# Two scatters, one gelu and four copies change their stage, and two loop heads change their order

## The chip, the cores and the metric

The kernel runs on one core of a Trainium2 chip. A core has five engines that run their own instruction streams and meet only at semaphores: TensorE (PE: matmuls), VectorE (DVE), ScalarE (ACT: activation functions and copies), GpSimd (POOL) and SyncE (SP: it issues DMA transfers). The metric is device time in microseconds (us), the median over several runs.

## The reference, cut to what matters

The reference is a transformer of two layers over 4 x 512 tokens of 128 channels. The part that matters is the attention of the first layer, with 16 heads and a window of 64 keys that slides over time:

```python
strain = disp_win - disp[:, :, :, None, :]             # 64 window places per token
bond_act = gelu(strain @ W_strain + rel_emb @ W_pos)   # exact gelu
damage_act = gelu(strain @ W_dmg + b_dmg)
logits = bond_act @ W_bond - 10.0 * sigmoid(damage_act @ W_dmg_out + b_dmg_out)
weights = softmax(where(cmask, logits, -inf))
out = einsum("bntd,bntde->bnte", weights, val_win)     # then W_cproj
```

Beside it stands a mixture of 16 experts of which each token uses 4: x + attention(xn) + experts(xn). The second layer (ordinary attention and 8 experts) is not touched by the change.

## The kernel before, in words

The first layer runs in five blocks, one after another: set-up, then for each of two groups of 8 heads (g = 0, 1) a loop and a band stage. At the end of a block all engines wait for each other.

**The loop.** It goes through the 64 window places j as items, eight to a body (`it`). For an item VectorE writes two halves, s = 0 (bond) and s = 1 (damage), into one of four ring slots (`strained`, line 261). For the items 1, 2, 4, 5 and 7 of a body TensorE makes the s = 1 half instead, in two half passes (`strain`, lines 999 and 1003) from `DS`, a copy of the data in three bfloat16 parts; ScalarE then takes the gelu of such an item in three pieces (lines 921, 922 and 924), of the others in one (line 916). TensorE reduces the gelus into logits (`reduce`, line 975), which frees the ring slot. Beside this run the experts' groups, four tiles of 128 rows each: SP loads rows (`tokens`) and weights, TensorE turns them and multiplies (`turn`, `hidden`, `expert_out`), VectorE moves and activates (`move_in`, `glu_in`, `glu_out`, `move_out`), and GpSimd scatters the results to DRAM with four indirect transfers a group (`store`, line 267). `MOE` says which groups a body handles: in the first loop groups 0 to 4, in its bodies 5, 6 and 7; in the second loop the other fifteen, in its bodies 0 to 7.

**The head of the first loop.** TensorE counts the tokens of each expert (`count`, `starts`), VectorE makes the tables (`expert_tiles`, `token_slots`, `tile_tables`), GpSimd scatters 64 sets of rows to the experts' order (line 770). The copies into `DS` (`send_parts`, line 256) are four transfers for each of three parts; parts 0 and 1 are sent by SP in set-up, part 2 in the loop.

**The band stage.** TensorE turns the logits, VectorE subtracts the maxima, ScalarE takes the exp, SP writes the result to DRAM (`band`), and SP and GpSimd read it back skewed, one half of the partitions each (`read`, line 1168), into three buffers (`wide`) that GpSimd clears first (line 1176). It clears `vp`, too, the tile for the values (line 1177). TensorE then turns and gathers what was read, for four blocks k of time steps. In the first band stage the other head group's data are prepared beside it, among them item 0 of the second loop (`strained` by VectorE in block 3), whose gelu opens the second loop.

What sets the order is each engine's own program, written out by hand; the semaphores only say how long it waits.

Of the kernel before, what the change touches and what calls it, by code (L numbers as in the profile page):

```python
# [20 lines left out]
P = 128  # L21
B, T, C = 4, 512, 128
NT = T // P
# [64 lines left out]
def first_step(j):  # L88

    return WIN - 4 - 4 * (j // 4)  # L90
# [91 lines left out]
def first_layer(nc, t_in, l0, sb, psum, sem, ident, ACC, nhalf, stats, mv, rstd, carried):  # L182
# [87 lines left out]
    with ExitStack() as su:  # L270
# [49 lines left out]
        def _(sp):  # L320
# [25 lines left out]
            send_parts(sp, 0, parts0, (1,))  # L346
# [293 lines left out]
    wide_zero, side_pe, side_sb = sem("wide_zero"), sem("side_pe"), sem("side_sb")  # L640
# [26 lines left out]
    for g in range(G):  # L667
        with ExitStack() as lp:
# [21 lines left out]
            def _(sp):  # L690
# [25 lines left out]
                if g == 0:  # L716
                    send_parts(sp, 0, parts0, (2,))
# [26 lines left out]
            def _(pool):  # L744
# [28 lines left out]
                for n in groups:  # L773
                    if n < groups[-1]:
                        goals(n + 1)
                    pool.wait_ge(goals_ready, n + 1)
                    if g or n < groups[-1]:
                        store(pool, n)

            @block.vector  # L780
            def _(v):
# [104 lines left out]
                if g == 0:  # L886
                    v.wait_ge(items_reduced, 1)
                    strain(0, 0, 0)
                    expert_tiles()
                    strain(0, 0, 1).then_inc(strain_ready, 1)  # L890
                    token_slots()
                item(1, 0)
                if g == 0:
                    tile_tables()
                item(2, 0)
# [9 lines left out]
            def _(act):  # L905
# [50 lines left out]
                gelu(0, 0)  # L956
# [5 lines left out]
            def _(pe):  # L962
                def reduce(n, it):
# [9 lines left out]
                    for s in range(2):  # L973
# [3 lines left out]
                    mm.then_inc(items_reduced, 1)  # L977
# [109 lines left out]
                strain(1, 0, 0)  # L1087
                if g == 0:
                    tables()
                strain(1, 0, 1)  # L1090
                reduce(0, 0)
                turn(moe_groups(g, 0)[0])
                strain(2, 0, 0)
# [9 lines left out]
        with ExitStack() as sm:  # L1103
# [52 lines left out]
            def read(engine, k, half, only=None):  # L1156

                engine.wait_ge(wide_zero, (WIDE + 1) * g + min(k, WIDE - 1) + 1)
# [13 lines left out]
            def _(pool):  # L1172
                if g == 0:
                    store(pool, MOE[0][7][1])
                for n in range(WIDE):
                    pool.memset(wide[n], 0.0).then_inc(wide_zero, 1)
                pool.memset(vp, 0.0).then_inc(wide_zero, 1)
                for k in range(NT):
                    read(pool, k, 1)
# [36 lines left out]
            def _(v):  # L1216
# [41 lines left out]
                for k in range(NT):  # L1258
# [7 lines left out]
                    if (g, k) == (0, 3):  # L1266
                        strained(v, ring[:, 0], 0, 1)
# [12 lines left out]
            def _(act):  # L1280
# [33 lines left out]

                weigh(0)
# [3 lines left out]
                act.wait_ge(wide_zero, (WIDE + 1) * (g + 1))  # L1319
                values(0)  # L1320
                for k in range(NT):
# [12 lines left out]
                    for i in sides(k)[1]:  # L1334
                        side(i)

# [1137 lines left out]
```

## Time and profile before

| | |
|---|---|
| time, median of 3 runs | 1234.41 us (1232.6 to 1237.3) |
| the profiled execution | 1235.36 us, its span 1233.6 us |
| set-up | 0 to 46.3 us |
| first loop, first band stage | 46.3 to 312.9, 312.9 to 395.0 us |
| second loop, second band stage | 395.0 to 655.9, 655.9 to about 750 us |
| busy over the span | PE 82%, DVE 73%, ACT 63%, POOL 45% |

All times of a row are us from the first instruction of the execution. A row of the timeline gives start, duration, engine, line, operation, what it writes and reads, and in brackets how long the engine stood idle before it and whose end released it. "issue" is a wait for nothing that the profile shows; "PEq" is a sequencer. An engine that is not the last to arrive at a point can be idle at no cost.

### The profile page before, as it was taken

What the parts mean: (1) busy time and instruction counts of PE and PEld (TensorE: products, weight loads), DVE (VectorE), ACT (ScalarE), POOL (GpSimd) and SP (SyncE); (2) the same over time, 40 slices, a digit from 0 to 9 for tenths busy, and PEclk for the clock granted to TensorE, in tenths of its full rate; (3) what the DMA queues carried; (4) which work ended last, traced back from release to release, by engine and by line L of the source; (5) the groups of instructions that cost most, each with busy time, mean ns of one, the idle gap of its engine ahead of it and who ended that gap; (6) DMA issues with size and microseconds to landing.
All of it is one profiled execution on the core that took longest, in us unless ns stands there. A gap on an engine that the chain in (4) does not pass through costs nothing. (4 is left out here: it accounts for less than half of the span.)

```text
span 1233.6 us, 24798 instructions
## 1 busy us (share of the span) xinstructions
PE 1016.2 (82%) x9866; PEld 547.7 (44%) x9866; DVE 894.7 (73%) x1046; ACT 783.0 (63%) x848; POOL 550.8 (45%) x571
## 2 busy tenths in 40 slices
PE   6687777898587988988885879987799999998557
PEld 4422222233566333333334868345345656464123
DVE  7778788997637899999986555684485776667137
ACT  3589999998544899999995322421465665555234
POOL 5188887067734188888876104057300000000720
PEclk9789999999799999999998889987699999899679
DMA  8840111021493122222206910002113435231110
GB/s 298 246 154 33 35 35 35 19 64 41 121 235 73 49 73 71 71 69 68 69 31 188 257 40 22 0 10 92 37 52 111 129 113 154 77 86 52 50 28 26
DMA packets 117418, 105.32 MB, mean 85 GB/s; under 512 B 11861, under 2 KB 103665, under 8 KB 116657
## 3 DMA queue, kind: packets, MB, share of 16 engines
q1 hardware_dynamic: 107220, 83.41, 24.1%
q0 software_dynamic: 8512, 20.13, 5.6%
q8 instruction: 78, 1.28, 0.4%
q10 hardware_dynamic: 1571, 0.20, 0.1%
q14 instruction: 37, 0.30, 0.1%
HBM read 62.16 MB, written 38.39 MB: 82 GB/s over the span
## 5 line engine op out<-in xcount | busy, mean ns | idle before, releaser
L261 DVE SCALAR_TENSOR_TENSOR ring<-AD,PT 128x1808 f32<-128x1808 f32 (+15 forms) x128 | 282.8, 2222 | 35.0 <-PE LG L975 20.2
L975 PE MATMUL LG<-ring,lred 128*32 128x456 f32 (+15 forms) x2048 | 238.5, 586 | 0.0
L2240 ACT ACTIVATE EX<-SS 128x1024 f32<-128x1024 f32 x128 | 130.8, 1030 | 122.7 <-PE SS L2027 80.0
L267 POOL DMA_INDIRECT ys<-rows,goali x80 | 160.8, 2010 | 106.9 <-DVE rows L861 76.1
L2310 DVE TENSOR_REDUCE MX<-SS 128x2 f32<-128x1024 f32 x119 | 144.5, 1218 | 71.7 <-PE SS L2027 50.5
L916 ACT ACTIVATE ring<-ring 128x3616 f32<-128x3616 f32 (+15 forms) x48 | 164.4, 3424 | 3.7 <-DVE ring L261 3.6
L999 PE MATMUL SD<-DSf,eyes 99*32 99x456 bf16 (+15 forms) x1280 | 95.9, 376 | 78.0 <-ACT ring L921 69.7
L922 ACT ACTIVATE ring<-ring 128x1824 f32<-128x1824 f32 (+15 forms) x80 | 145.7, 1821 | 0.0
L1944 POOL DMA_INDIRECT XN<-ys,sloti x16 | 16.6, 1040 | 269.3 <-PE SS L2037 264.7
L770 POOL DMA_INDIRECT xs<-rows,sloti x64 | 122.1, 1907 | 30.2 <-issue 19.2
L975 PEld LDWEIGHTS LG<-ring,lred 128*32 128x32 f32 x2048 | 61.8, 112 | 100.6 <-issue 78.8
L261 DVE SCALAR_TENSOR_TENSOR ring<-AD,bdmg 128x1808 f32<-128x1808 f32 (+15 forms) x48 | 106.4, 2217 | 0.0
L999 PEld LDWEIGHTS SD<-DSf,eyes 99*32 99x32 bf16 x1280 | 21.2, 95 | 179.8 <-ACT ring L921 111.6
L921 ACT ACTIVATE ring<-SD 128x912 f32<-128x912 f32 (+15 forms) x80 | 78.3, 979 | 30.3 <-PE SD L1003 17.4
L1003 PE MATMUL SD<-DSf,eyes 96*32 96x456 bf16 (+15 forms) x1280 | 95.4, 374 | 0.0
L2027 PE MATMUL SS<-QS,KS 32*128 32x512 f32 x256 | 67.8, 530 | 28.1 <-ACT EX L2240 21.1
L924 ACT ACTIVATE ring<-SD 128x912 f32<-128x912 f32 (+15 forms) x80 | 78.5, 981 | 10.0 <-PE SD L1003 9.9
L2027 PE MATMUL SS<-KS,QS 32*128 32x512 f32 x238 | 63.2, 518 | 14.5 <-DVE MX L2310 12.5
L2047 PE MATMUL PW<-EX,VA 128*32 128x512 f32 x512 | 73.4, 649 | 0.0
L2217 ACT ACTIVATE HB<-PHh,b1c 128x128 f32<-128x128 f32 x156 | 44.7, 371 | 41.3 <-PE PHh L1979 41.3
L2362 DVE RECIPROCAL attT<-attT 128x128 f32<-128x128 f32 (+1 forms) x58 | 54.5, 959 | 0.2
L2027 PEld LDWEIGHTS SS<-QS,KS 32*128 32x128 f32 x256 | 25.3, 195 | 64.0 <-ACT EX L2240 30.9
(417 smaller groups left out, 1751.1 us busy)
## 6 DMA issues: line engine op xcount, KB each, us to landing
w1s<-in_L_ffn_W SPq DMA_DIRECT2D x39, 256.0 KB
w2s<-in_L_ffn_W SPq DMA_DIRECT2D x39, 256.0 KB
band<-ring SPq DMA_DIRECT2D x6, 1024.0 KB, 9.5
xl<-xs SPq DMA_DIRECT2D x20, 272.0 KB, 3.1
xs<-Z SPq DMA_DIRECT2D x5, 1024.0 KB, 8.5
w1s<-w1d SPq DMA_DIRECT2D x80, 64.0 KB
w2s<-w2d SPq DMA_DIRECT2D x80, 64.0 KB
band<-Z SPq DMA_DIRECT2D x4, 1024.0 KB
```

Of the source, the lines that this page charges most:

```text
L261: return v.scalar_tensor_tensor(out=tile[:, s, :, t0:T], in0=AD[:, s, :, j + t0:j + T], scalar=extra, in1=AD[:, s, :, PAD + t0:PAD + T], o ...
L267: pool.indirect_dma_start(ys0[:, :], bass.IndirectOffsetOnAxis(ap=goali[:, 4 * n + a:4 * n + a + 1], axis=0), yo[:, n % 2, a, :], None, bo ...
L770: pool.indirect_dma_start(xs0[:, :], bass.IndirectOffsetOnAxis(ap=sloti[:, t, k:k + 1], axis=0), rows[:, t, :], None, bounds_check=ROWS0 - ...
L916: act.activation(tiles, tiles, ACT.Gelu).then_inc(gelu_done, 1)
L922: act.activation(tiles, tiles, ACT.Gelu)
L924: act.activation(ring[:, slot, 1, 2:4, t0:T], SD[:, :, t0:T], ACT.Gelu).then_inc(gelu_done, 1)
L975: mm = pe.matmul(LG[32 * b:32 * b + 32, par, s, t0:T], lred[:, s, n % 4, :], ring[:, slot, s, b, t0:T], start=(n % 4 == 0), stop=(n % 4 == 3))
L999: pe.matmul(SD[32 * q:32 * q + 32, i, t0:T], eyes[0:99, q, :], DS[0:99, q, 2 * half + i, j + t0:j + T], start=True, stop=False)
L1003: mm = pe.matmul(SD[32 * q:32 * q + 32, i, t0:T], eyes[0:96, 4, :], DS[0:96, q, 2 * half + i, PAD + t0:PAD + T], start=False, stop=True)
L2027: mm = pe.matmul(bank[:, n, :], rows[r:r + 32, b % 2, q, P * t:P * t + P], cols[r:r + 32, b % 2, q, :], start=True, stop=True)
L2240: act.activation(EX[:, Q % 2, hh:hh + 2, t, :], SS[:, slot, :, :], ACT.Exp, scale=SCALE1).then_inc(freed[slot], 1)
L2310: v.tensor_reduce(MX[:, t, p // 2, hh:hh + 2], pairs_of(b, name), AX.X, ALU.max).then_inc(freed[slot], 1)
```

## The change: what it does

- `send_parts` for part 1 goes from SP's set-up to SP's first loop, beside part 2.
- The head of the first loop: VectorE computes item 1 ahead of `token_slots`, and item 2 ahead of `tile_tables`. TensorE puts `tables` behind the second half of item 1's strain, and the reduction of item 0 behind the first half of item 2's.
- The first loop's last two scatters (groups 3 and 4; of these group 4's was in the band stage already) both stand in the first band stage, each behind one clear; the clear of the third buffer and the later reads come after them. The clear of `vp` goes to ScalarE as a copy of a zero column, ahead of its exps, in both band stages.
- The gelu of the second loop's item 0 is done at the end of the first band stage by ScalarE, in two pieces (s = 1, then s = 0); VectorE signals the first piece by a semaphore of its own.
- The head of the second loop: TensorE splits the reduction of item 0 in two (s = 0 before, s = 1 behind the second half of item 1's strain), and turns the experts' rows behind the first half of item 2's strain.

```diff
@@ set-up, SP
-            send_parts(sp, 0, parts0, (1,))
@@ first loop, SP
-                    send_parts(sp, 0, parts0, (2,))
+                    send_parts(sp, 0, parts0, (1, 2))
@@ loops, GpSimd
-                    if g or n < groups[-1]:
+                    if g or n < groups[-2]:
                         store(pool, n)
@@ loops, VectorE
-                    token_slots()
                 item(1, 0)
                 if g == 0:
+                    token_slots()
+                item(2, 0)
+                if g == 0:
                     tile_tables()
-                item(2, 0)
@@ loops, ScalarE
-                gelu(0, 0)
+                if g == 0:
+                    gelu(0, 0)
                 gelu(1, 0)
@@ loops, TensorE
-                def reduce(n, it):
+                def reduce(n, it, which=(0, 1)):
...
-                    for s in range(2):
+                    for s in which:
...
-                    mm.then_inc(items_reduced, 1)
+                    if which[-1]:
+                        mm.then_inc(items_reduced, 1)
...
                 strain(1, 0, 0)
+                if g:
+                    reduce(0, 0, (0,))
+                strain(1, 0, 1)
+                if g:
+                    reduce(0, 0, (1,))
+                else:
+                    tables()
+                strain(2, 0, 0)
                 if g == 0:
-                    tables()
-                strain(1, 0, 1)
-                reduce(0, 0)
+                    reduce(0, 0)
                 turn(moe_groups(g, 0)[0])
-                strain(2, 0, 0)
                 strain(2, 0, 1)
@@ band stages, GpSimd
+                def clear(n):
+                    pool.memset(wide[n], 0.0).then_inc(wide_zero, 1)
+
+                clear(0)
+                if g == 0:
+                    store(pool, MOE[0][7][0])
+                clear(1)
+                read(pool, 0, 1)
                 if g == 0:
                     store(pool, MOE[0][7][1])
-                for n in range(WIDE):
-                    pool.memset(wide[n], 0.0).then_inc(wide_zero, 1)
-                pool.memset(vp, 0.0).then_inc(wide_zero, 1)
-                for k in range(NT):
+                clear(2)
+                for k in range(1, NT):
                     read(pool, k, 1)
@@ band stages, VectorE
-                        strained(v, ring[:, 0], 0, 1)
+                        strained(v, ring[:, 0], 0, 1).then_inc(parts_dve, 1)
@@ band stages, ScalarE
+                act.copy(vp.rearrange("p a n h e -> p (a n h e)"), xnT[:, 0, 0:1].to_broadcast([P, 2 * 8 * HG * 32])).then_inc(vp_zero, 1)
                 weigh(0)
...
-                act.wait_ge(wide_zero, (WIDE + 1) * (g + 1))
+                act.wait_ge(vp_zero, g + 1)
...
+                if g == 0:
+                    for s, ready, count, done in ((1, parts_dve, 5, parts_act), (0, strain_ready, 65, gelu_done)):
+                        tiles = ring[:, 0, s, :, first_step(0):T]
+                        act.wait_ge(ready, count)
+                        act.activation(tiles, tiles, ACT.Gelu).then_inc(done, 1)
```

## Rows read from the trace of the kernel before

**Rows 1.** Busy time by stretch: start:end, length, PE, PEld, DVE, ACT, POOL, PE clock.

```profile
46.30:69.50 23.20, 17.83 (x168) 10.80 (x168) 17.95 (x36) 11.18 (x9) 11.47 (x15) 0.74 1.04 327
69.50:299.00 229.50, 188.66 (x2252) 66.49 (x2252) 196.50 (x127) 215.85 (x155) 160.16 (x109) 0.97 0.13 41
...
410.50:653.00 242.50, 215.52 (x2508) 89.85 (x2504) 226.39 (x201) 226.20 (x169) 185.96 (x151) 1.00 0.21 62
```

**Rows 2.** VectorE's waits in the second loop: us in total, times, longest.

```profile
DVE rows L861 <- PE PY L1054: 8.1, 8, 2.4
```

**Rows 3.** Timeline, set-up into the first loop: start, us, instruction, idle before.

```profile
41.08 4.55 SPq L256 DMA_DIRECT2D DSf<-tT  x4
...
46.33 2.10 DVE L261 SCALAR_TENSOR_TENSOR ring<-AD,PT 128x1808 f32<-128x1808 f32 x1 [2.99 <-PEq L270]
...
46.36 2.68 SPq L256 DMA_DIRECT2D DSf<-XN  x4
```

**Rows 4.** Timeline, the edges behind the loops and into the second loop.

```profile
293.92 2.55 POOL L267 DMA_INDIRECT ys<-rows,goali  x1 [0.30 <-issue]
...
305.10 0.97 POOL L267 DMA_INDIRECT ys<-rows,goali  x1 [0.30 <-issue]
...
312.96 1.23 DVE L1218 TENSOR_TENSOR Z<-Z,mz 128x1024 f32<-128x1024 f32 x1 [4.95 <-PEq L668]
...
395.03 6.13 DVE L261 SCALAR_TENSOR_TENSOR ring<-AD,PT 128x1808 f32<-128x1808 f32 x3 [0.32 <-PEq L1103]
...
649.72 0.98 POOL L267 DMA_INDIRECT ys<-rows,goali  x1 [0.31 <-issue]
...
655.93 1.23 DVE L1218 TENSOR_TENSOR Z<-Z,mz 128x1024 f32<-128x1024 f32 x1 [2.65 <-PEq L668]
```

**Rows 5.** Timeline, head of the first loop.

```profile
51.22 3.22 ACT L916 ACTIVATE ring<-ring 128x3616 f32<-128x3616 f32 x1 [3.65 <-DVE ring L261]
...
54.87 0.42 DVE L817 SCALAR_TENSOR_TENSOR chosen_key<-PH,chosen_key 128x256 f32<-128x256 f32 x1 [3.68 <-PE PH L1023]
...
55.16 0.56 PE L1003 MATMUL SD<-DSf,eyes 96*32 96x452 bf16 x8
...
59.84 0.93 ACT L921 ACTIVATE ring<-SD 128x904 f32<-128x904 f32 x1 [5.41 <-DVE ring L261]
...
60.66 1.71 ACT L922 ACTIVATE ring<-ring 128x1808 f32<-128x1808 f32 x1
...
62.31 3.06 PE L975 MATMUL LG<-ring,lred 128*32 128x452 f32 x16
...
68.02 1.69 PE L975 MATMUL LG<-ring,lred 128*32 128x452 f32 x16
...
69.48 3.22 ACT L916 ACTIVATE ring<-ring 128x3616 f32<-128x3616 f32 x1
```

**Rows 6.** Timeline, first band stage.

```profile
318.86 3.53 POOL L1176 MEMSET ring<- 128x4096 f32 x1
...
319.16 2.05 ACT L1287 ACTIVATE ring<-wtT 128x1024 f32<-128x1024 f32 x1 [4.95 <-issue]
...
336.18 1.17 POOL L1168 DMA_DIRECT2D DSf<-band  x2 [1.13 <-DMA band<-ring]
...
357.56 1.11 PE L1384 MATMUL WB<-ident,DSf 128*128 128x128 f32 x8
...
389.96 2.10 DVE L261 SCALAR_TENSOR_TENSOR ring<-AD,PT 128x1808 f32<-128x1808 f32 x1
```

**Rows 7.** A scatter in the first loop; the four in the band stage, grouped.

```profile
61.24 7.79 POOL L770 DMA_INDIRECT xs<-rows,sloti  x1 [0.31 <-issue]
...
L267 POOL DMA_INDIRECT ys<-rows,goali x4 | 4.3, 1074 | 8.5 <-POOLq L668 7.6 <-issue 0.9
```

**Rows 8.** Transfers of 333 to 353 us: count, KB each, us to landing.

```profile
DSf<-band POOLq DMA_DIRECT2D x2, 380.0 KB, 9.4
```

**Rows 9.** Timeline, head of the second loop.

```profile
410.81 2.12 DVE L261 SCALAR_TENSOR_TENSOR ring<-AD,PT 128x1824 f32<-128x1824 f32 x1 [1.94 <-PE LG L975]
```

More of the change, by code:

```diff
@@ L639, in first_layer @@
         sem(n) for n in ("band_pe", "band_act", "band_dve", "vw_pe", "vw_sb", "nd_pe", "rc_ready", "att_ready"))
-    wide_zero, side_pe, side_sb = sem("wide_zero"), sem("side_pe"), sem("side_sb")
+    wide_zero, vp_zero, side_pe, side_sb = sem("wide_zero"), sem("vp_zero"), sem("side_pe"), sem("side_sb")
     def fetch(sp, k):
@@ L1156, in read @@
             def read(engine, k, half, only=None):
-                engine.wait_ge(wide_zero, (WIDE + 1) * g + min(k, WIDE - 1) + 1)
+                engine.wait_ge(wide_zero, WIDE * g + min(k, WIDE - 1) + 1)
                 if k >= WIDE:
```

## The prediction, made before the changed kernel ran

> **What bounds the kernel now.** I read the split of the span by stage first, then who waits for whom inside the two loops, then the timeline around each edge between stages. In the first loop's steady part ScalarE is busy 215.85 of 229.5 us, VectorE 196.5; in the second loop's 226.20 and 226.39 of 242.5, and of VectorE's 16 us without work 8.1 are waits for the expert outputs on TensorE [rows 1, 2]. So the first loop ends when ScalarE's row of gelus ends, the second when VectorE's or ScalarE's does: work that hides elsewhere is worth nothing, and what such a loop can be given is an earlier start. The change touches exactly the starts: two heads and two edges. The timeline shows how much is idle there.
>
> **Edge from set-up into the first loop.** VectorE stood idle 2.99 us before its first instruction at 46.33, while SP issued the four copies of the second part until 45.63 (41.08 + 4.55) [rows 3]. With the copies moved behind the edge, VectorE is last, with its end at 43.34. How fast an edge is when nothing holds it shows at the one into the second loop: VectorE idle 0.32 us [rows 4]; from SP's end to 46.33 it is 0.70. The edge falls at 43.7 to 44.0: 2.3 to 2.6 us won. The copies are not gone: SP now issues eight in a row, at 0.67 us each (46.36: 2.68 for four) to 1.14 (41.08) [rows 3]: 5.4 to 9.1 us. TensorE's first strain matmuls, which wait for them, end at 55.72 and start about 1 us earlier, behind the counting of tokens [rows 5], 8.4 us after the edge. Their cover is that counting. At 0.67 us each 3.0 us remain for landing, at 1.14 they are 0.7 us late plus the landing, which no row gives alone; so the term lies between 0 and 2.6. The 1.14 belongs to copies that queue behind set-up's weight transfers; these get 2.7 us more, so I take the nearer row, 0.67, and **2.3**. The zero stores and expert weights behind them on SP move by about as much; the expert groups begin in the sixth body, over 100 us later.
>
> **Head of the first loop.** ScalarE ends its first gelu at 54.44, then idles 5.41 us before the second item's first piece; the first gelu in one piece after that, item 3's, starts at 69.48 [rows 5]. The 5.41 us are a wait for VectorE's item 1, which stands behind the token slots, for which VectorE itself idled 3.68 us (before 54.87). In the new order item 1 (2.1 us, the mean of three in 6.13 us [rows 4]) runs in that gap, 51.2 to 53.3. Then, in the clock of before: strain matmuls until 55.72; gelu 1's first half 0.93 us until 56.7; second strain half about 1.0 until 57.7; ScalarE's other two pieces 1.7 and 0.93 until 59.3; strain of item 2 until 60.3, its first half gelu until 61.2; the delayed first reduction (1.69 us at the full clock, row 68.02) until 62.0, second strain half until 63.0, gelu 2 ends 63.9. VectorE: token slots end at 57.7 as before (item 1 now ends behind them at 59.8), item 2 59.8, tables 60.3, item 3 (two pieces) 64.4. So gelu 3 starts at 64.4 in place of 69.48: 5.1 us. The doubt is TensorE's clock: its granted mean in this head is 0.74 against 0.97 behind it [rows 1], and the same reduction took 3.06 us at 62.31, behind two idle stretches of some 2.1 us: there it ran at 1.2 in place of 2.4 GHz. Were all these matmuls at the lower level, the same walk gives 66.8, thus 2.7. The new gaps are each 1.1 us or less, so the full clock is nearer: **4.6**, between 2.7 and 5.1.
>
> **Edge out of the first loop.** VectorE idles 4.95 us before the band stage, from 308.01 [rows 4]. GpSimd's last scatter ended at 306.07 (305.10 + 0.97), 6.9 us before. At the end of the second loop, where its last scatter ended at 650.70, 5.2 us before, the idle time is 2.65. At the edge into the second loop, with no scatter near, it is 0.32. I read it as GpSimd arriving 5 to 7 us after a scatter. In the new kernel the last scatters before this edge are group 2's, which end at 296.5, 11.5 us before 308.01. Then VectorE is last: 4.95 less 0.32 to 0.70 gives 4.2 to 4.6, **4.4**; below, 0, if something else holds the edge.
>
> **Band stage.** Three things are added. ScalarE clears the value tile (128 x 4096) in GpSimd's place: the gelu of 3,616 elements took 3.22 us [rows 5], so 3.7; ScalarE's first exp waits until 319.16, 6.2 us into the stage, of which its wait for VectorE is the last 4.95 [rows 6]. Cost 0, cover 1.2 us even if what stands before that wait stays. ScalarE's moved gelu is two pieces of 1.7 us, the second after VectorE's strain piece at 392.06 (389.96 + 2.10); it ends near 393.9, before VectorE's last piece at 394.7 [rows 4, 6]: cost 0, cover 0.8. GpSimd's order becomes clear, scatters, clear, first read, scatters, clear, reads. A scatter there takes 1.07 us on average, a group with its issue gaps 5.2 [rows 7]. The first read, behind 3.5 + 5.2 + 3.5 = 12.2 us, is earlier than now (behind two more clears); the second, now issued at 336.18, 23.3 into the stage, falls at 23.3 to 25. It needs 9.4 us to land [rows 8] and TensorE turns it at 357.56: 10 us of cover. **0**.
>
> The price of a scatter is the place where the stage could turn. A scatter in the first loop took 7.79 us at 61.24 [rows 7], across VectorE's unbroken row of strain pieces. The Trainium skill, "SBUF — State Buffer", section "SBUF: two separate sides", says that a VectorE operation with two inputs in SBUF and a GpSimd operation that reads SBUF exclude each other for the whole instruction. By that rule the 7.79 belongs to the strain pieces, the band stage's reductions and subtractions, which read PSUM, would not stretch a scatter, and the term stays 0; the 1.07 agrees. Without it a busy DMA queue would be the other reading, the one priced in the last rival.
>
> **Head of the second loop.** VectorE's item 5 starts at 410.81, 15.8 us into the stage, after 1.94 us of waiting for TensorE's reduction 1 [rows 9]; ScalarE's gelu 1 stands behind gelu 0. With gelu 0 done, ScalarE starts on gelu 1 when item 1 is there (395.03 + 2.05 = 397.1): its pieces until 398.0, 399.7, 400.7; strain of item 2 until 401.9; gelu 2's pieces 402.8, 404.5, 405.4; gelu 3 at 405.4. Reduction 1 follows the second strain half (404.0) and ends 405.7: item 5 at 405.9 in place of 410.81, 4.9 us. At the lower clock gelu 3 starts at 406.8 and item 5 at 409.1, 1.7 earlier. VectorE is as full as ScalarE here [rows 1], so its figure counts. Half of the reduction of item 0 now stands in one of TensorE's gaps, none over 1.1 us; I take **4.2**.
>
> **Sum.** 2.3 + 4.6 + 4.4 + 0 + 4.2 = 15.5 us. The profiled execution took 1235.36 (its span 1233.6 and 1.76 around it), 0.95 above the median of the runs: 1219.9 against it, 1218.9 against the median 1234.41. That is the forecast. Its own bounds: least 0 + 2.7 + 4.2 + 1.7 = 8.6 (1225.8), most 2.6 + 5.1 + 4.6 + 4.9 = 17.2 (1217.2).
>
> **Rivals.** (a) The edge out of the first loop keeps its 4.95 us, since not GpSimd holds it. For: TensorE's side also idles there, and the last scatter's 64 KB cannot take 6 us to move. Against: the two edges of rows 4 that are slow are the two with a scatter 5 to 7 us before, and the idle times shrink together. Time 1218.9 + 4.4 = 1223.3. The Trainium skill, "DMA: Bandwidth & Descriptors", section "Anatomy of one DMA — SWDGE (gpsimd) path", gives about 2.0 us fixed per GpSimd transfer, mostly the write's receipt. By that figure, as an estimate, GpSimd would be done near VectorE's end at 308, which speaks for (a); the 6.9 us of the row speaks against its being all.
> (b) The loops hand the heads back: a later meeting with expert weights or GpSimd's queue sets their end. For: the 8.1 us of waits for expert outputs [rows 2]. Against: those waits hang on work that itself moves with the loop. Time: only the edges count, 6.7 us, 1227.7.
> (c) Slower: a scatter in the band stage stretches to the 7.79 us of row 61.24. Eight of them put 8 x 6.7 = 54 us before the second read, less its 10 us of cover: 44 us at TensorE's turns, net 1263. It decides from a stretch of 15.5 + 10 = 25.5 us on, 4.3 us a scatter. Against: the 1.07 us of four in this stage.
>
> **How the numbers follow.** Forecast 0.66, (a) 0.14, (b) 0.15, (c) 0.05. The three runs of before spread over 4.7 us, 2.4 to a side. The range goes from the forecast's best less that, 1214.5, to 1228.0, which holds the forecast's worst with the spread, (a), and half of (b); out stay (c), the other half of (b) and a few hundredths. About 0.5%, 6.2 us, is what a measurement of this kernel can tell from no change: faster (below 1228.2) has the forecast, (a) and half of (b), 0.86; same 0.10; slower 0.04.
>
> **What would show it.** Right: VectorE's first instruction of the first loop near 43.9; gelu 3 some 18 us after it instead of 23; the idle time at the edge into the band stage under 1 us; scatters there near 1.1 us; item 5 in the second loop about 10.9 us after its edge instead of 15.8; both loops' steady parts as long as before. Wrong: VectorE waiting for the parts' copies, TensorE at 1.2 GHz in the heads, 2 us or more of it at the band's edge, TensorE waiting for a read at its first two turns, or steady parts that grew by what the heads lost.

## The result, and the profile after

The changed kernel took 1217.52 us (median of four runs, 1214.8 to 1219.91) where the kernel before took 1235.86 beside it: ratio 0.986, interval 0.9834 to 0.9886, 18.3 us less. The forecast was 1218.9. The profiled execution took 1217.04, its span 1215.3. The stages run from VectorE's first instruction in one to its first in the next:

| stage | before | after | won | forecast |
|---|---|---|---|---|
| set-up | 46.33 | 43.63 | 2.70 | 2.3 |
| first loop, its edge out included | 266.63 | 256.53 | 10.10 | 4.6 + 4.4 |
| first band stage | 82.07 | 79.03 | 3.04 | 0 |
| second loop | 260.90 | 255.37 | 5.53 | 4.2 |
| all behind it | 577.67 | 580.74 | -3.07 | 0 |

Of the first loop's 10.10 us the head has 4.08 (up to item 3's gelu, 23.15 us behind the edge before and 19.07 after), the edge out 4.63, and 1.39 lie between the two. That stretch, from item 3's gelu to VectorE's end, takes 236.9 to 238.5 us in the fourteen executions of the table below (238.53 before, 237.14 after), so the 1.39 us are no more than one execution differs from the next.

Busy time by stretch, with the columns of [rows 1]: the head of the first loop, its steady part, the steady part of the second loop.

```profile
43.60:62.70 19.10, 17.23 (x164) 11.23 (x168) 16.62 (x36) 11.19 (x9) 7.11 (x14) 0.75 1.01 285
62.70:289.00 226.30, 181.60 (x2230) 63.13 (x2223) 196.92 (x124) 212.83 (x154) 176.12 (x103) 0.99 0.16 52
389.00:630.00 241.00, 215.10 (x2508) 89.78 (x2504) 226.74 (x201) 225.58 (x168) 194.71 (x162) 1.00 0.22 64
```

VectorE is busy 196.92 us in the 226.3 us of the first loop's steady part, 196.50 in the 229.5 us taken before [rows 1]: about the same work, at an earlier time. The head still has a granted clock of 0.75 (0.74 before). The timeline of the changed kernel at its heads and edges:

```profile
43.63 2.10 DVE L261 SCALAR_TENSOR_TENSOR ring<-AD,PT 128x1808 f32<-128x1808 f32 x1 [0.32 <-PEq L270]
43.66 2.54 SPq L256 DMA_DIRECT2D DSf<-tT  x4
46.24 2.55 SPq L256 DMA_DIRECT2D DSf<-XN  x4
...
52.63 0.57 PE L1001 MATMUL SD<-DSf,eyes 99*32 99x452 bf16 x8
...
57.09 0.94 PE L1001 MATMUL SD<-DSf,eyes 99*32 99x452 bf16 x8 [0.67 <-ACT ring L924]
58.57 2.47 PE L976 MATMUL LG<-ring,lred 128*32 128x452 f32 x16
59.10 13.90 POOL L769 DMA_INDIRECT xs<-rows,sloti  x1 [0.30 <-issue]
62.70 3.21 ACT L916 ACTIVATE ring<-ring 128x3616 f32<-128x3616 f32 x1
...
300.12 3.54 POOL L1181 MEMSET ring<- 128x4096 f32 x1 [9.03 <-POOLq L667]
300.16 1.23 DVE L1231 TENSOR_TENSOR Z<-Z,mz 128x1024 f32<-128x1024 f32 x1 [0.32 <-PEq L667]
300.16 1.94 PE L1365 MATMUL ZT<-ident,Z 128*128 128x128 f32 x16 [1.65 <-PEq L667]
302.14 1.23 DVE L1240 TENSOR_REDUCE mx<-ZT 128x16 f32<-128x1024 f32 x1 [0.75 <-PE ZT L1365]
303.82 1.10 POOL L267 DMA_INDIRECT ys<-rows,goali  x1 [0.16 <-issue]
...
320.64 7.45 PE L143 MATMUL ZT<-ident 128*128 128x128 f32 x40 [0.84 <-DVE wtT L1242]
...
376.48 1.71 ACT L1354 ACTIVATE ring<-ring 128x1808 f32<-128x1808 f32 x1 [0.26 <-DVE ring L261]
379.19 6.13 DVE L261 SCALAR_TENSOR_TENSOR ring<-AD,PT 128x1808 f32<-128x1808 f32 x3 [0.32 <-PEq L1110]
387.54 1.69 PE L976 MATMUL LG<-ring,lred 128*32 128x452 f32 x16
387.86 4.13 DVE L261 SCALAR_TENSOR_TENSOR ring<-AD,PT 128x1824 f32<-128x1824 f32 x2
389.01 3.22 ACT L916 ACTIVATE ring<-ring 128x3616 f32<-128x3616 f32 x1
392.95 2.11 DVE L261 SCALAR_TENSOR_TENSOR ring<-AD,PT 128x1824 f32<-128x1824 f32 x1
...
634.56 1.23 DVE L1231 TENSOR_TENSOR Z<-Z,mz 128x1024 f32<-128x1024 f32 x1 [2.63 <-PEq L667]
```

What to see: the first two slow edges of [rows 3, 4] now have VectorE idle 0.32 us in place of 2.99 and 4.95, the third keeps its 2.63 (2.65 before). Item 3's gelu stands 19.07 us behind the first edge (62.70 - 43.63), 23.15 before [rows 5]. At the edge into the band stage TensorE's first sixteen turns take 1.94 us and VectorE's first maximum follows 1.98 behind the edge; before it was 3.65 and 3.68. In the second loop item 5, the second of the two pieces at 387.86, starts at 389.88, 10.69 us behind the edge, 15.78 before [rows 9]; item 6 stands 13.76 behind it, 19.28 before. The lines of the first band stage before that these readings need, and two that are taken up below:

```profile
312.96 3.65 PE L1346 MATMUL ZT<-ident,Z 128*128 128x128 f32 x16 [7.18 <-PEq L668]
316.64 1.23 DVE L1227 TENSOR_REDUCE mx<-ZT 128x16 f32<-128x1024 f32 x1 [2.46 <-PE ZT L1346]
...
335.14 6.15 PE L143 MATMUL ZT<-ident 128*128 128x128 f32 x40 [1.46 <-DVE wtT L1229]
...
370.35 1.20 PE L1410 MATMUL ZT<-wtT,ring 128*32 128x64 f32 x67 [3.44 <-issue]
```

### The profile page after: what moved, and what is told of

The parts are those of the page before. It is cut to its first block and busy times, and to the rows that moved or that the text cites. A ratio compares the mean times of both kernels' runs of the same rounds, so it can differ in the third digit from the quotient of the medians.

```text
span 1215.3 us, 24799 instructions
## 1 busy us (share of the span) xinstructions
PE 1012.9 (83%) x9866; PEld 549.0 (45%) x9866; DVE 894.8 (74%) x1046; ACT 790.0 (65%) x851; POOL 563.5 (46%) x569
## 3 DMA queue, kind: packets, MB, share of 16 engines
q8 instruction: 78, 1.28, 0.4%
## 5 line engine op out<-in xcount | busy, mean ns | idle before, releaser
L976 PE MATMUL LG<-ring,lred 128*32 128x456 f32 (+15 forms) x2048 | 232.5, 573 | 0.0
L916 ACT ACTIVATE ring<-ring 128x3680 f32<-128x3680 f32 (+15 forms) x47 | 161.2, 3430 | 3.6 <-DVE ring L261 3.6
L769 POOL DMA_INDIRECT xs<-rows,sloti x64 | 134.4, 2099 | 30.7 <-issue 19.2
L924 ACT ACTIVATE ring<-SD 128x912 f32<-128x912 f32 (+15 forms) x80 | 78.5, 982 | 10.2 <-PE SD L1005 10.2
```

The costliest lines, as they stand in the source:

```text
L769: pool.indirect_dma_start(xs0[:, :], bass.IndirectOffsetOnAxis(ap=sloti[:, t, k:k + 1], axis=0), rows[:, t, :], None, bounds_check=ROWS0 - ...
L916: act.activation(tiles, tiles, ACT.Gelu).then_inc(gelu_done, 1)
L976: mm = pe.matmul(LG[32 * b:32 * b + 32, par, s, t0:T], lred[:, s, n % 4, :], ring[:, slot, s, b, t0:T], start=(n % 4 == 0), stop=(n % 4 == 3))
```

## The experiments

The total moves by some 2 us to either side from run to run, as much as one part of the change is worth; so the parts are told apart by the stage lengths of the profiled executions, one of each kernel (us). The kernels e5 to e10 ran once, the others four to six times:

| kernel | set-up | first loop | idle at its edge | first band stage | second loop | behind |
|---|---|---|---|---|---|---|
| before | 46.33 | 266.63 | 4.95 | 82.07 | 260.90 | 577.67 |
| changed | 43.63 | 256.53 | 0.32 | 79.03 | 255.37 | 580.74 |
| e1 | 43.51 | 263.23 | 5.00 | 81.55 | 255.00 | 575.71 |
| e2 | 42.18 | 258.13 | 0.32 | 79.45 | 252.64 | 580.30 |
| e3 | 43.11 | 261.12 | 0.33 | 78.25 | 254.81 | 576.71 |
| e4 | 43.93 | 258.18 | 0.32 | 79.67 | 259.91 | 576.61 |
| e5 | 43.36 | 262.81 | 5.71 | 81.48 | 252.67 | 574.18 |
| e6 | 43.89 | 266.66 | 7.95 | 85.73 | 256.43 | 574.69 |
| e7 | 43.65 | 257.35 | 0.33 | 77.51 | 255.34 | 577.05 |
| e8 | 43.16 | 258.42 | 0.33 | 78.68 | 257.36 | 575.08 |
| e9 | 42.99 | 259.43 | 2.67 | 80.08 | 255.05 | 578.85 |
| e10 | 45.73 | 257.67 | 0.33 | 77.84 | 256.59 | 577.87 |
| e11 (changed again) | 43.34 | 258.41 | 0.33 | 79.11 | 254.91 | 575.63 |
| e12 | 43.50 | 256.44 | 0.32 | 78.12 | 253.58 | 581.46 |

### e1: one group's scatters back in the loop

```diff
-                    if g or n < groups[-2]:
+                    if g or n < groups[-1]:
                         store(pool, n)
@@ band stage
                 clear(0)
-                if g == 0:
-                    store(pool, MOE[0][7][0])
```

> Group 3's four scatters stand in the first loop again, all else as changed. Theory (GpSimd passes the end of a block only some 5 to 7 us after its last indirect scatter): VectorE's idle time at the edge into the first band stage returns from 0.32 to 4.4 to 5.0 us. On the 3.0 us that the first band stage gained without being forecast: if TensorE's slow first turns (3.65 us before, 1.94 after) come from its standing idle at that edge, they return too and VectorE's first maximum stands 3.7 us behind the edge; together 4.4 to 7.4 us, 1221.9 to 1224.9. Rival (a), something else held that edge: idle 0.3 to 0.5, time unchanged, 1217.5. Rival on the band stage, the new order of clears and reads made its gain: the stage stays at 79.0 us even with the idle edge.

Measured: 1221.15 us (ratio to before 0.9911, 0.9881 to 0.9941). The edge idles 5.00 us again, and TensorE's slow turns are back. Timeline, TensorE and VectorE at the edge:

```profile
306.74 3.65 PE L1363 MATMUL ZT<-ident,Z 128*128 128x128 f32 x16 [7.18 <-PEq L667]
306.74 1.23 DVE L1229 TENSOR_TENSOR Z<-Z,mz 128x1024 f32<-128x1024 f32 x1 [5.00 <-PEq L667]
310.43 1.22 DVE L1238 TENSOR_REDUCE mx<-ZT 128x16 f32<-128x1024 f32 x1 [2.46 <-PE ZT L1363]
```

So rival (a) falls: the edge does hang on GpSimd. (Only these four scatters changed their block; group 4's stood in the band stage before, too.) The time lies a little under the 1221.9 to 1224.9 that were expected. The stage behind the idle edge takes 81.55, though the new order of clears and reads is nearly all there; of the 2.52 us over the changed kernel's 79.03, 0.57 are there when TensorE begins to turn what was read (28.34 us behind the edge, 27.77), and 1.85 are a longer stall at "issue" in the first gather (3.26 for 1.41), which may not come from the edge.

### e2: the second loop's last scatters moved too

```diff
-                    if g or n < groups[-2]:
+                    if n < groups[-1] if g else n < groups[-2]:
                         store(pool, n)
@@ band stage, GpSimd
+                if g:
+                    store(pool, MOE[1][7][0])
                 clear(0)
@@ band stage, SP
+                write(0)
+                read(sp, 0, 0, 0)
                 if g == G - 1:
...
                     fetch(sp, 0)
                     fetch(sp, 1)
-                write(0)
-                read(sp, 0, 0, 0)
```

> The second loop's last four scatters (group 19) also go into the stage behind it, ahead of its first clear; SP waits for them and fetches the experts' rows behind its first two reads in place of ahead of its first write. Theory (scatters hold the edge): VectorE's idle time at the edge into the second band stage falls from 2.63 to 0.3 to 0.7, the stage behind it stays at 94.3 us up to the second layer, the time falls by 2.0 to 2.3 to 1215.3. Rival: something else holds that edge (TensorE's last expert product): idle stays near 2.6 and the time with it. Second rival: the later fetch is late for VectorE's additions of the experts' rows, which start 22.05 us into the stage now; if they start 2 us or more later, the gain is gone.

Measured: 1214.74 us (ratio 0.9853, 0.9813 to 0.9892). The first theory holds at the third edge too (idle 0.32, the loop 2.3 to 2.7 us shorter), but the stage behind it, up to the second layer's first matmul, takes 97.55 us where the changed kernel has 94.26 and 94.85. VectorE's additions are on time (20.33 us into the stage). SP is what is late: its second write to DRAM stands behind the fetch. SP's issues, and ScalarE's last exp, which needs that write's buffer:

```profile
643.67 0.81 SPq L642 DMA_DIRECT2D rows<-ys  x1
644.92 2.16 SPq L642 DMA_DIRECT2D fetched<-ys  x1
647.78 6.56 SPq L1205 DMA_DIRECT2D band<-ring  x1
654.44 3.03 SPq L1175 DMA_DIRECT2D ring<-band  x2
...
661.19 3.87 ACT L1302 ACTIVATE ring<-wtT 128x2048 f32<-128x2048 f32 x1 [8.90 <-DMA band<-ring]
```

That write's issue took 0.59 us in the changed kernel. The exp waits 8.90 us for it, and ScalarE's copies for TensorE's turns stand behind the exp. The edge's gain went into SP's queue, which none of the theories had named; the time can't be told from the changed kernel's (ratio 0.986).

### e3: the first loop's head in its old order

```diff
+                if g == 0:
+                    token_slots()
                 item(1, 0)
                 if g == 0:
-                    token_slots()
+                    tile_tables()
                 item(2, 0)
-                if g == 0:
-                    tile_tables()
```

(and TensorE's `tables`, `reduce` and `turn` back in their old places for g = 0).

> The first loop's head in the order of before on VectorE (token slots ahead of item 1) and TensorE (tables and the reduction ahead of item 2's strain), all else as changed. Theory: ScalarE's first gelu in one piece (item 3) goes from 19.1 us behind the edge back to 23.2, VectorE idles 3.7 us ahead of the token slots again, the loop grows from 256.5 to 260.6 and the time by 4.1 to 1221.6. Rival (b): a later meeting sets the loop's end and the loop grows by less than 2 us.

Measured: 1218.26 us (ratio 0.9885, 0.9856 to 0.9914). Item 3's gelu stands 23.42 us behind the edge, VectorE idles 3.86 ahead of the token slots, and the loop takes 261.12. The executions with the new order and no other edit in the head have item 3 at 19.07 to 20.78, mean 20.02 over the nine of them, and the five of these whose edge isn't held have loops of 256.5 to 258.4. So the order is worth some 3.4 us at item 3 and 2.7 to 4.6 at the loop's end: nothing is handed back. The time was expected at 1221.6; by the ratios, 0.9885 against the changed kernel's 0.986, the old head costs some 3 us, with intervals that overlap.

### e4: the second loop's head undone; e8: only TensorE's order there undone

```diff
@@ e4: band stage and loop, ScalarE
-                if g == 0:
-                    for s, ready, count, done in ((1, parts_dve, 5, parts_act), (0, strain_ready, 65, gelu_done)):
...
-                if g == 0:
-                    gelu(0, 0)
+                gelu(0, 0)
@@ e4 and e8: loop, TensorE
                 strain(1, 0, 0)
-                if g:
-                    reduce(0, 0, (0,))
                 strain(1, 0, 1)
                 if g:
-                    reduce(0, 0, (1,))
+                    reduce(0, 0)
+                    turn(moe_groups(g, 0)[0])
...
                 strain(2, 0, 0)
```

> Item 0's gelu is back in the second loop and TensorE's reduction there is unsplit in its old place, all else as changed. Theory: item 6 goes from 13.8 us behind the edge back to 19.3 and the loop grows from 255.4 to 260.9, time plus 5.5: 1223.0; the first band stage, where the gelu ends 0.7 us ahead of VectorE, stays at 79.0. Rival (b): the loop's end is set by a later meeting and grows by less than 2 us. Second rival: the gelu in the band stage does cost something there, and that stage gets shorter by up to 4.7 us, so that less than 5.5 is lost.

> As changed, item 0's gelu stays in the band stage, but TensorE's order in the second loop's head is that of before (reduction of item 0 whole, then the turn, then item 2's strain). Theory: the moved gelu is worth most of the 5 us; at the full clock item 2's first strain half ends 0.8 us later and the loop grows by 0.9; if TensorE's clock falls in its then longer gap (2.0 us ahead of item 1's second half), by up to 2.5. Rival: order and gelu are worth half each, the loop grows by over 2.5 us.

Measured: e4 1217.99 us (ratio 0.9867, 0.983 to 0.9904), its loop 259.91, which is 4.8 over 255.1, the mean of the nine executions that have this loop as changed (252.7 to 256.6); item 3's gelu stands 14.47 us behind the edge, in the nine at 10.2 on the mean (9.8 to 11.2). The time was expected at 1223.0; by the ratios (0.9867, 0.986) the total lost only 0.9 us, within intervals of 3 to 5 us to either side, so that it neither shows the 4.8 us nor speaks against them. The band stage is not shorter (79.67), so the moved gelu costs nothing there. e8 1214.40 us, its loop 257.36, 2.2 over the same mean, item 3 at 12.36. Timeline of e8, TensorE:

```profile
380.41 0.81 PE L1001 MATMUL SD<-DSf,eyes 99*32 99x452 bf16 x8 [2.72 <-PEq L1109]
380.97 1.00 PE L1005 MATMUL SD<-DSf,eyes 96*32 96x452 bf16 x8
383.37 0.95 PE L1001 MATMUL SD<-DSf,eyes 99*32 99x452 bf16 x8 [1.39 <-ACT ring L921]
384.10 0.97 PE L1005 MATMUL SD<-DSf,eyes 96*32 96x452 bf16 x8
384.85 2.96 PE L976 MATMUL LG<-ring,lred 128*32 128x452 f32 x16
```

With the old order TensorE's granted clock is 0.54 behind its gap, close to its lower level of 1.2 GHz, with the strain half at 0.95 us and the reduction at 2.96; in the changed kernel the half reduction stands in that gap, the clock is 1.00, the strain half takes 0.57 and the two halves of the reduction 0.95 and 0.93.

But the order is not all of it: e8's clock is 0.56 in the two rows ahead of the gap already, where its program is still that of the changed kernel. The clock falls in this head with the new order as well, in e5 and e6 to 0.50 and 0.51, and item 3 stands at 11.17 and 11.16 there, against 9.8 at the full clock. So the order is worth 1.2 us at item 3 with the clock alike, and 2.5 where it also saves the clock; the gelu, between e4 and e8, which are both at the lower clock from the first row on, 2.11 at item 3 and 2.55 at the loop's end. About half each is what one execution of either says, and the nine loops spread over 3.9 us.

### e5, e9: a clear in place of the scatters

```diff
                     if g or n < groups[-2]:
                         store(pool, n)
+                    elif n == groups[-2]:
+                        pool.wait_ge(y_used, n + 1)
+                        for a in range(6):  # e9: 3
+                            link(pool.memset(fetched[:, 0:8, :], 0.0))
```

> As changed (both last groups' scatters stay in the band stage), but where group 3's four scatters stood in the first loop GpSimd clears a tile that nothing reads, six times, 5 to 6 us in all, with the same wait ahead of it. Theory (it is the scatters, the indirect transfers, that hold the edge): VectorE's idle time at the edge stays at 0.3 and the first loop at 256.5 to 258.2 us. Rival: any work of GpSimd's that late holds the edge: idle 4 to 5 us, the loop at 261 to 263.

Measured: 1216.19 us; the edge idles 5.71 us and the loop takes 262.81. My theory fell: it is not the scatter just before the edge. Timeline, GpSimd and VectorE:

```profile
293.41 6.00 POOL L781 MEMSET fetched<- 128x1024 f32 x6 [1.63 <-DVE rows L864]
306.12 3.52 POOL L1185 MEMSET ring<- 128x4096 f32 x1 [6.71 <-POOLq L667]
306.17 1.23 DVE L1235 TENSOR_TENSOR Z<-Z,mz 128x1024 f32<-128x1024 f32 x1 [5.71 <-PEq L667]
```

And the view of the transfers from 299.5 to 306, the stretch behind the last clear:

```profile
DMA packets 0, 0.00 MB, mean 0 GB/s; under 512 B 0, under 2 KB 0, under 8 KB 0
```

No transfer is under way at all, and all other engines ended 5.71 us or more ahead of the edge. So GpSimd is late by itself. The same with half as many clears:

> The run with the tile cleared in place of the scatters, with three clears in place of six, so that GpSimd's last operation ends 3.0 us earlier. New theory (GpSimd passes this edge a fixed 6.7 to 6.9 us after its last operation in the loop, whatever operation that is): GpSimd's last clear still ends 6.7 to 6.9 us ahead of the edge, VectorE idles 2.6 to 2.9 us in place of 5.7. Rival (the edge is late for another reason that the clears bring about, such as their wait for VectorE): idle stays at 5 to 6 us, or goes to 0.3.

```profile
292.70 2.97 POOL L781 MEMSET fetched<- 128x1024 f32 x3 [1.63 <-DVE rows L864]
302.38 3.51 POOL L1185 MEMSET ring<- 128x4096 f32 x1 [6.71 <-POOLq L667]
302.42 1.23 DVE L1235 TENSOR_TENSOR Z<-Z,mz 128x1024 f32<-128x1024 f32 x1 [2.67 <-PEq L667]
```

Measured: 1218.14 us. Three us less of clears, three us less of idle time (5.71 to 2.67), and GpSimd again 6.71 us from its last operation to its first behind the edge. The new theory holds.

What GpSimd does in these 6.71 us stands in the trace, among the rows of its sequencer at the block's end: one instruction, DRAIN. A row gives its time in ns (least, median, most) and its start in us; the first three are the edge out of the first loop in the changed kernel, in e1 and in e5, the others the edge out of the second loop in the changed kernel and in e2:

```profile
L667 POOLq DRAIN  x1: 6263/6263/6263, 291.4 to 291.4; - x1
L667 POOLq DRAIN  x1: 10372/10372/10372, 296.1 to 296.1; - x1
L667 POOLq DRAIN  x1: 6263/6263/6263, 299.6 to 299.6; - x1
...
L667 POOLq DRAIN  x1: 8414/8414/8414, 625.9 to 625.9; - x1
L667 POOLq DRAIN  x1: 11686/11686/11686, 614.6 to 614.6; - x1
```

It can begin while scatters still run, as in e1; counted from the end of GpSimd's last operation it goes by the number of indirect scatters that GpSimd issued in the whole block. It is 6.60 us for 80 of them (before, e1, e6), 6.26 for 76 (the changed kernel, e5, e9), 4.95 for 60 and 4.63 for 56 (e2, e12) out of the second loop, and 5.28 or 5.29 for 64 in the program's last block, of the second layer: 0.0825 us each. So the scatters do set the time, all those of the block, and the clears only move its start. The four scatters that the change takes out of the block shorten its DRAIN by only 0.34 us; the edge is free since GpSimd's last operation now ends 9.03 us ahead of GpSimd's first behind it.

### e6: TensorE kept busy at the slow edge

```diff
                 expert_out(moe_groups(g, 7)[1])
+                if g == 0:
+                    keep_busy(pe, SD[:, 0, 0:P], ident, 44)
```

(on top of e1).

> Group 3's scatters back in the first loop (the edge idles 5.0 us), and TensorE runs 44 matmuls of zero use behind its last expert product, some 5.4 us, into the 7.2 us in which it stood idle there. Theory (the first band stage's unforecast gain is TensorE's clock, which fell in that idle time): the edge stays at 5.0, but the first 16 turns of the band stage take 1.94 in place of 3.65 us, VectorE's first maximum stands 2.0 behind the edge in place of 3.7, turn 0 some 26.6 in place of 28.3. Rival (the slow first turns come from something else at an edge behind scatters): they stay at 3.65.

Measured: 1229.12 us. The filler was longer than I reckoned (9.99 us) and held the edge itself, VectorE idle 7.95; so this run tells of the clock alone:

```profile
310.55 1.94 PE L1365 MATMUL ZT<-ident,Z 128*128 128x128 f32 x16 [0.30 <-PEq L667]
```

With TensorE at work up to the edge its first turns take 1.94 us at a granted clock of 1.00, though VectorE idled 7.95; in e1, where TensorE idled 7.18, they take 3.65 at 0.50, in e9, where it idled 4.00, 3.58 at 0.53. It is the clock. At the turn of what was read 1.06 us of the 1.7 are left (27.28 us behind the edge, 28.34 in e1; 26.6 were expected), and the stage as a whole got longer (85.73): its first gather stalls 3.85 us at "issue" (3.26 in e1), and the matmuls behind it are slower (2.08 us for two that take 1.13 in e1).

### e7: TensorE kept busy in the first loop's head

```diff
+                if g == 0:
+                    keep_busy(pe, LG[:, 1, 0, 0:P], ident, 8)
                 strain(1, 0, 1)
...
                     tables()
+                    keep_busy(pe, LG[:, 1, 0, 0:P], ident, 10)
```

> As changed, with TensorE matmuls of no use in two gaps of the first loop's head: 8 between the two halves of item 1's strain, 10 behind the tables. Theory (the head's term was missed by 0.5 to 1.7 us since TensorE ran at its lower clock there, first reduction 2.5 to 3.2 us in place of 1.69): the reduction takes 1.7 to 1.9 and ScalarE's item 3 stands 17.8 to 18.4 us behind the edge in place of 19.1 to 20.4, the forecast's 18; the loop is 0.9 to 2 us shorter (255 to 256.5). Rival: the fillers only delay what stands behind them (up to 2 us), item 3 at 19 to 22. Second rival: the reduction is faster but the loop's end stays where it was, 256.5 to 258.2.

Measured: 1212.67 us, but item 3 at 20.00 and the loop at 257.35, both within the others' range. Busy time and granted clock, first of this kernel from its first strain half on:

```profile
52.50:56.90 4.40, 4.36 (x53) 3.03 (x52) 4.22 (x24) 2.69 (x3) 0.93 (x1) 1.00 1.08 383
56.90:62.00 5.10, 5.10 (x62) 3.44 (x64) 5.00 (x6) 2.33 (x3) 4.80 (x2) 1.00 1.07 367
```

and the same stretches of the changed kernel:

```profile
52.60:57.10 4.50, 2.66 (x41) 1.13 (x40) 4.22 (x24) 3.34 (x3) 0.95 (x1) 0.96 1.09 385
57.10:61.00 3.90, 3.90 (x36) 1.34 (x40) 3.90 (x5) 2.10 (x2) 3.60 (x2) 0.61 1.06 364
```

The clock stays at 1.00 and the first reduction takes 1.69 us in place of 2.47, as the theory says; but the fillers take 2.05 and 2.50 us in gaps of 1.09 and 0.67, and what they delay eats what the clock gives: the first rival.

### e10: the copies back in set-up

```diff
             sp.dma_start(w2d.rearrange("e p c -> p e c"), w2T[:]).then_inc(d_small, 16)
+            send_parts(sp, 0, parts0, (1,))
...
-                    send_parts(sp, 0, parts0, (1, 2))
+                    send_parts(sp, 0, parts0, (2,))
```

> The copies of part 1 back in SP's set-up, all else as changed. Theory: SP is the last at the first edge again, VectorE's first instruction of the first loop goes from 43.6 (42.2 to 43.9 in the runs so far) to some 46.3 behind 3 us of idle time, and the loop keeps its length, 256.5 to 258.4: the copies hid behind the counting of tokens. Rival: the copies cost the loop's head something in their new place, and the loop is 1 us or more shorter without them.

Measured: 1217.47 us. SP issues its four copies in 3.78 us and ends 0.69 ahead of the edge, VectorE idles 2.21, set-up takes 45.73: 2.4 us over e11. The loop is 257.67, no shorter than the others. In their new place the copies are not quite free: TensorE's first strain half stands 8.25 us behind the edge here, 8.9 to 9.0 in all the others but before (8.43), and where the counting was quick TensorE waits for them: 0.47 in e11, 1.42 in e12, 1.49 in e8.

### e11, e12: the changed kernel again, and the best guess

e12 is e2 with fewer fillers than e7 (4 and 2 matmuls).

> The changed kernel itself, for its time beside the next one on one chip, and for how far its stages move from run to run: first loop 256.5 to 258.4, first band stage 78 to 80, second loop 254.8 to 255.4, all behind it 574 to 581 us. The theory that the 3.1 us which the part behind the second loop lost by the first profile is run-to-run variation and not the change wants that part anywhere in 574 to 581 again; that it is the change wants 580 to 581.

> The second loop's last scatters behind its edge, as in the run of that alone, and fewer filler matmuls in the first loop's head than before: 4 between the halves of item 1's strain (1.0 us at the full clock), 2 behind the tables (0.5). Theory: VectorE's idle time at the second edge is 0.3 (2.3 us won), TensorE keeps its full clock through the head, the first reduction takes 1.69 us and ScalarE's item 3 stands 17.8 to 18.3 us behind the edge in place of 19.1 to 20.8; together 3.3 to 4.5 us under the changed kernel's time on the same chip. Rival: so few fillers don't hold the clock (reduction 2.5 to 3.2), or the loop's end doesn't follow its head: 2.3 us.

Measured: e11 1212.81 us (ratio 0.9866, 0.9836 to 0.9897), e12 1215.44 (0.9873, 0.984 to 0.9906), before 1230.65 beside both. The part behind the second loop is 575.63 in e11: the 3.07 us that it lost in the first profile are variation from run to run, as other kernels that leave it alone have 574.2 to 578.9. e12 is not faster than the change. Its third edge idles 0.32, but the stage behind it takes 97.24, as in e2. In its head the first four fillers took 2.05 us where I had reckoned 1.0, and item 3 stands at 19.18: the reduction is fast (1.69) and the gain is spent, as in e7. No kernel here beats the changed one measurably.

## Why the prediction was right, point by point

**The time.** Forecast 15.5 us won; the medians give 18.3 and, repeated, 17.8 (1230.65 - 1212.81). The parts were right in sign and place: the four terms give 2.70 + 4.08 + 4.63 + 5.53 = 16.9 us in the profiled executions, the second head more than forecast, the first head less. That the total lies as near is in part luck: the first band stage (3.04) and the first loop's steady part (1.39) add 4.4 that the sum did not have, and the part behind the second loop, which differs that much from run to run, takes 3.07 away. Two sums of the range are 0.2 to 0.3 off: 1217.2 less 2.4 is 1214.8 and 1225.8 with the spread 1228.2; nothing hangs on it.

**Set-up, 2.3: measured 2.7**, 2.4 between e10 and e11. The copies' cover was nearly exhausted: the wait of 0 to 1.5 us for them in the head, which the prediction priced at 0 behind the nearer of its two rows, is there.

**Head of the first loop, 4.6: measured 4.08 in the profile, 3.1 on the mean of nine (23.15 - 20.02; 3.4 against e3).** The step that failed is "the new gaps are each 1.1 us or less, so the full clock is nearer". The gaps were 1.09 and 0.67 us and the clock behind them is 0.61, the reduction 2.47 us (to 3.23 in the nine) for 1.69, so on the mean the walk at the lower clock (2.7) was nearer than the one at the full clock (5.1). Some 0.5 us is not the clock: TensorE's first strain half already starts 0.57 us later behind the edge than before (9.00 for 8.43), held by the counting in this execution and by the copies in others. e7 shows that the full clock can be had by filling the gaps, and that this costs what it gives.

**Edge out of the first loop, 4.4: measured 4.63**, 4.7 undone in e1. The size is right and rival (a) fell; the reason given was nearly right. "GpSimd arriving 5 to 7 us after a scatter" is GpSimd arriving 6.7 to 6.9 us after its last operation of any kind at this edge (e5, e9), with no transfer under way, since its DRAIN takes 0.0825 us for every scatter that the block has issued; that is also why the edge out of the second loop, with 60 scatters for 80, comes after 5.2 us. The Trainium skill, "DMA: Bandwidth & Descriptors", section "Anatomy of one DMA — SWDGE (gpsimd) path", and its 2.0 us a transfer therefore don't bear on this edge: e5 waits as long with no packet moving.

**First band stage, 0: measured 3.04.** The costs were at zero, as priced: ScalarE's clear (3.64 us) and the table load behind it (1.28) let the first exp start 0.47 us after VectorE's subtraction, and the wait of 2.44 us ahead of the third exp takes that up. What the sum lacked is a gain. TensorE idled 7.18 us at the slow edge, as e1 shows again, and started the stage at its lower clock, VectorE's maxima behind it: 1.7 us (3.68 to 1.98), undone in e1 and shown to be the clock in e6. The stage takes 81.5 to 82.1 where the edge idles 4.95 to 5.71 (before, e1, e5), 80.1 at 2.67 (e9) and 77.5 to 79.7 at 0.3.

But most of the 1.7 us is lost again inside the stage: TensorE begins to turn what was read 27.77 us behind the edge, 28.17 before, only 0.40 us earlier, since the clock fell once more in the waits for VectorE (0.50 from 307 to 316) and the 20 filler matmuls ahead of that turn took 7.45 us in place of 6.15. Over the executions 1.1 us is left: 28.13 to 28.34 behind the slow edge (before, e1, e5), 27.11 on the mean of the nine with an edge of 0.3. The other 2.64 us arise behind that turn, where before TensorE stalled 3.44 us at "issue" in the second gather and the changed kernel didn't. Such stalls add up to 0.5 to 3.2 us a stage in the nine, to 5.1, 3.4, 3.6 and 4.6 in before, e1, e5 and e6 and to 1.2 in e9; whether a slow edge lengthens them is not shown.

**The scatters' price there.** They took 0.97 to 1.10 us, and rival (c) fell. The Trainium skill, "SBUF — State Buffer", section "SBUF: two separate sides" (VectorE operations with two inputs in SBUF shut out GpSimd operations that read it) agrees with the trace here, and in the first loop's head more strikingly: the scatter at 59.10 took 13.90 us, to 73.00, beside a row of VectorE's two-input pieces without a gap from 57.89 to 72.13. In e11, where that row has three gaps of 0.2 to 0.5 us, five scatters ran in the same time, the first of them 3.75 us. In both kernels, and at 61.24 before, each of these scatters ends 0.84 to 0.87 us behind the end of one of VectorE's pieces; why GpSimd got its turn at two places without a gap in e11, and at none of six such places in the changed kernel, is not shown.

**Head of the second loop, 4.2: measured 5.53**, 4.8 undone in e4. TensorE kept its full clock here (1.00), so the walk's upper bound of 4.9 was the right end: item 5 came 10.69 us behind the edge in place of 15.78, 5.1 us. That the clock holds is not sure: in e5 and e6 it fell in this head, and item 3 came 1.35 us later. The order, with the half reduction in the gap, is worth 1.2 to 2.5 us by itself (e8). With the gelu went ScalarE's table load of 1.28 us, which the prediction does not name: it stood at 394.99, in the head of the loop, before, and stands at 373.20, inside the band stage, after.

**Rival (b)** fell: both loops kept their heads (e3, e4).

## What to carry to other kernels

An engine off the critical path can set a block's end by when its last operation ends, well after that operation: look at each slow edge for the engine that comes last, read what its sequencer does there, and move its last work behind the edge or ahead of the others' end. With GpSimd that means its last operation's end plus 0.0825 us for each indirect scatter of the block. A term that shortens an idle time of TensorE can also give back clock in the stage behind, and should be priced at both levels and followed to the stage's end; a term at its best case is not the likeliest. A transfer moved on SP is priced with what stands behind it in SP's queue: e2 won 2.3 us at an edge and lost 3 in the stage behind it, with SP's queue late.

## What the runs showed of the hardware that was not expected

GpSimd needed 6.7 to 6.9 us from its last operation to the edge into the first band stage, whether that was a scatter (e1: ended 299.86, edge 306.74) or a clear (e5, e9), and 5.23 or 5.24 us at the edge out of the second loop, behind a scatter, in all twelve executions that have it there. The difference is the number of scatters in the block, 80 or 76 against 60: the DRAIN at its end takes 0.0825 us for each, and no transfer needs to be under way. In the set-up, where GpSimd issues no transfer, it ends 0.05 us after the last operation. In the band stages, where GpSimd issues ten plain reads, the count of scatters is not enough: 1.21 us in the first with four scatters, 1.53 with eight, and 11.8 to 13.2 in the second. What the DRAIN does for each transfer is not shown. With GpSimd's last operation 9 us ahead it holds nothing up.

TensorE's first gather in the first band stage stalls at "issue" behind one and the same matmul, its 54th, in eleven of the fourteen executions, for 0.86 to 3.26 us (1.41 before and after the change). The timeline has no cause for it, but the transfers have: all 28 stalls of 0.15 us and more at "issue" that TensorE has in this stage in the fourteen executions end 1.2 to 1.7 us after a transfer of 16 KB has landed on the queue that the profile calls "instruction" (before, the stall of 3.44 us until 370.35: one from 367.38 to 368.75). So TensorE most likely waits there for its own program; why that transfer is late in one execution and not in another is not shown.
